# State-space heads: the parts of the third gate step all stand one pair of heads later

## The reference

```python
x = x + mamba2(gate0(x, f, f));  x = x + moe(gate1(x, f, f))
x = x + attention(gate2(x, f, f));  x = x + ffn(gate3(x, f, f))
```

```python
ek, ekv = exp(min(k, 30)), exp(min(k, 30)) * v
nf, df = scan forward of (ekv, ek) with a * decay + new      # along the 512 tokens
nb, db = the same scan backward
num = nf + nb - ekv + euk * v;  den = df + db - ek + euk     # euk = exp(min(u + k, 30))
out = sigmoid(r) * num / max(den, 1e-8) * (0.8 + 0.2 * tf)
```

```python
z, xBC, dt = split(u @ in_proj.T);  xBC = silu(conv4(xBC));  x, B, C = split(xBC)
L = tril(exp(cs_l - cs_s))            # per head, cs: running sum of dt * A in blocks
Y = (C B^T * L) (x dt) + C state * exp(cs) + x * D
y = Y * silu(z);  out = rmsnorm(y) * norm_w @ out_proj.T
```

## Time and profile before

| What | us |
|---|---|
| median of 3 runs | 2552.84 (2552.5 to 2559.88) |
| profiled execution, its own time | 2558.35 |
| its span in the trace | 2556.5 |
| DVE busy in the span | 1874.8 (73%) |
| PE busy in the span | 2282.6 (89%) |
| mean granted TensorE clock | 0.964 of full speed |

### The profile page before, as it was taken

One profiled execution on the slowest core, in us unless ns is written; L12 is line 12 of the kernel. 1 busy time (PEld: TensorE's weight loads), 2 busy tenths in 40 slices (PEclk: granted clock), 3 DMA queues, 4 the chain that ended last, 5 costly groups with the idle time before them and its releaser, 6 DMA issues.

```text
span 2556.5 us, 34018 instructions
## 1 busy us (share of the span) xinstructions
PE 2282.6 (89%) x10567; PEld 1688.2 (66%) x10568; DVE 1874.8 (73%) x2875; ACT 944.6 (37%) x1956; POOL 683.2 (27%) x545
## 2 busy tenths in 40 slices
PE   0789989989897899899878999999999988999998
PEld 0344444444455678778666888888888876788886
DVE  8989898889896765676545668768777785666665
ACT  3243342342432232342343444444434444322222
POOL 5434434343341443335331012122212210000000
PEclk9999999999998899999988999999999998999999
DMA  5000001010023432343241000010010101000001
GB/s 207 17 34 33 33 17 50 17 41 25 33 83 130 144 115 82 114 149 114 101 158 34 1 33 17 17 38 21 17 38 21 49 17 50 25 25 25 25 12 66
DMA packets 50502, 142.19 MB, mean 56 GB/s; under 512 B 4768, under 2 KB 4768, under 8 KB 46064
## 3 DMA queue, kind: packets, MB, share of 16 engines
q1 hardware_dynamic: 31872, 89.89, 10.0%
q10 hardware_dynamic: 12864, 32.81, 3.5%
q0 software_dynamic: 5680, 18.62, 2.4%
HBM read 106.95 MB, written 34.34 MB: 55 GB/s over the span
## 4 chain that ended last, share of the span: by engine, by line
PE 42%; issue 30%; POOL 10%; DVE 8%; POOLq 6%; ACT 3%; ACTq 0%; DMA 0%; DVEq 0%; another core or an unknown queue 0%
PE bank L341 9%; PE bank L343 9%; PE bank L342 9%; PE bank L2351 3%; PE bank L2352 3%; PE bank L2350 3%; PE bank L2304 3%; POOLq L494 2%; POOL g_v L495 2%; POOL g_v L502 2%; POOLq L520 1%; POOLq L517 1%; POOLq L506 1%; PE bank L2414 1%; POOL g_eu L501 1%
## 5 line engine op out<-in xcount | busy, mean ns | idle before, releaser
L2179 PE MATMUL bank<-um,w_in 128*128 128x512 f32 x576 | 263.5, 612 | 5.5 <-DVE lm L1515 5.3
L2179 PEld LDWEIGHTS bank<-um,w_in 128*128 128x128 f32 x576 | 110.0, 196 | 136.7 <-issue 128.5
L341 PE MATMUL bank<-u_hi,aw_hi 128*128 (+1 forms) x384 | 158.6, 413 | 12.9 <-DVE u_lo L1920 9.1
L1135 ACT ACTIVATE probs<-bank,nmx 128x128 f32<-128x128 f32 (+3 forms) x256 | 131.8, 528 | 91.6 <-DVE nmx L1943 91.6
L1142 ACT ACTIVATE pt_hi<-bank 128x512 fp32r<-128x512 f32 (+1 forms) x192 | 94.0, 526 | 165.0 <-PE bank L2304 163.8
L343 PE MATMUL bank<-u_hi,aw_lo 128*128 (+1 forms) x384 | 152.1, 396 | 0.0
L342 PE MATMUL bank<-u_lo,aw_hi 128*128 (+1 forms) x384 | 151.9, 396 | 0.0
L1958 DVE TENSOR_TENSOR pt_lo<-bank,pt_hi 128x512 fp32r<-128x512 f32 (+1 forms) x192 | 108.7, 593 | 42.5 <-ACT pt_hi L1142 41.1
L341 PE MATMUL bank<-u_hi,fw_hi 128*128 128x512 f32 x352 | 136.9, 389 | 0.0
L342 PE MATMUL bank<-u_lo,fw_hi 128*128 128x512 f32 x352 | 136.9, 389 | 0.0
L343 PE MATMUL bank<-u_hi,fw_lo 128*128 128x512 f32 x352 | 136.9, 389 | 0.0
(11 more groups left out here) (388 smaller groups left out, 6202.3 us busy)
## 6 DMA issues: line engine op xcount, KB each, us to landing
m_stage<-in_moe SPq DMA_DIRECT2D x21, 1024.0 KB, 5.3
y_slot<-m_o ACTq DMA_DIRECT2D x39, 256.0 KB, 2.7
g_v<-in_fT SPq DMA_DIRECT2D x18, 512.0 KB, 3.3
gates<-g_v SPq DMA_DIRECT2D x18, 512.0 KB, 2.8
f_stage<-in_ffn SPq DMA_DIRECT2D x11, 768.0 KB, 4.3
u_g<-gates SPq DMA_DIRECT2D x8, 1024.0 KB, 10.7
aw_in<-in_att SPq DMA_DIRECT2D x4, 1280.0 KB
w_in<-in_w_in ACTq DMA_DIRECT2D x1, 4640.0 KB, 16.8
```

Of the source, the lines that this page charges most:

```text
L341: nc.tensor.matmul(out, hi_w, hi_x, start=start, stop=False)
L1135: A(probs[:, h % 2, PR_AT[qb]:PR_AT[qb] + w], S_[bk][:, c0:c0 + w], ACT.Exp, bias=nmx[:, h % 2, qb:qb + 1], scale=SCALE, accum_out=rsum[:, ...
L2179: mm = M(dst[:], w_in[:, k, c0:c0 + P], um[:, k, :], start=(k == 0), stop=(k == KC - 1))
```

## The change

Each piece of the third gate step moves behind the output of the next pair of heads. The reciprocal, which stood behind pair 6, now stands behind pair 7, ahead of the two clamps of the fourth step, which stay where they were.

```diff
-                    if j == 0:
+                    if j == 1:
                         clamp(third, 0)
-                    elif j == 1:
+                    elif j == 2:
                         forward(third, 0)
                         clamp(third, 1)
-                    elif j == 2:
+                    elif j == 3:
                         backward(third, 0)
-                    elif j == 3:
+                    elif j == 4:
                         forward(third, 1)
-                    elif j == 4:
+                    elif j == 5:
                         backward(third, 1)
-                    elif j == 5:
+                    elif j == 6:
                         dens(third)
-                    elif j == 6:
+                    elif j == 7:
                         inverse(third)
-                    elif j == 7:
                         clamp(fourth, 0)
                         clamp(fourth, 1)
                 scans(fourth, 0)
```

## The result

The changed kernel takes **2590.62 us** (median of 4 runs, 2585.68 to 2593.72) against 2554.45 for the kernel before on the same chip (4 runs, 2552.5 to 2559.88): ratio 1.0137, 95% interval 1.0118 to 1.0156. Forecast were 2576.4 us and a range of 2567 to 2584. The direction was right, the size too small by more than the range allows.

The account below looks back on a forecast made before the run. DVE's own list was taken to bound each trip, PE's out_proj ending within 0.8 us of it; 5.9 us in each of four sequences, 23.6 us, on the 2552.84 us median gave 2576.4 us, range 2567 to 2584.

Parts of the forecast that it names:

- The chain in the loop: Each sequence's third to fourth gate step: the late reciprocal delays result, exponentials, products and scans, by 5.9 us a sequence.
- 4 x 5.9 = 23.6: Whole kernel: the 5.9 us delay counted in each of four sequences, 23.6 us added to the median.
- own range: Forecast case's range, 2571 to 2582 us, from the clamps' bounds and some 3 us of scatter; chance 0.74.
- the lower level does not fall on pair 2: Rival: PE finishes pair 2 at about 191.6, taking 1.6 us a sequence off: 17.2 us, 2570; chance 0.05.
- In the last sequence the same chain leads through the scans to the last additions to x, with which the mixture's routing begins: End of the last sequence: the delay there counts like the other three, 5.9 us.
- a wait of 3.4 us for DVE ahead of each *next trip: Trip's start: PE waits 3.4 us for DVE, so PE's own 1.7 us loss does not add.
- The rival on PE's clock: PE's clock falls in new gaps, slowing pair 7 by 1.5 us a sequence: 29.6 us, 2582; chance 0.07.
- The unknown at the clamps and POOL: Fourth step's clamp meeting POOL's first result: taken as zero more, bounds -0.3 and +0.7 us a sequence.
- The price of a meeting: POOL's result instruction meeting a DVE clamp: costs POOL 0.3 us or so, 1.61 us against 1.27.
- Faster, by the clamps: Rival at masked(2): tile 0's clamps gone, DVE gains 2.15 us a sequence plus a 0.53 us stall: -10.7 us, 2542; chance 0.05.

## Why the prediction was right in the loop and wrong in the sum

- *The chain in the loop* (DVE's stalls of 4.4, 2.2 and 1.8 us, the reciprocal 5.86 us late, 5.9 us a sequence): right. The stretch is 5.67 to 5.72 us longer in the first three and 6.03 in the fourth, 23.11 for 23.6. The reciprocal is 6.06 us late for 5.86, and the chain behind it, taken as unchanged at 9.31, is 0.41 us shorter. Moved alone, the reciprocal brings 4.12 of the 5.67; but the other pieces moved without it bring 3.95, so that it is not the reciprocal's place alone that counts.
- *"4 x 5.9 = 23.6"* as the loop's whole loss: 20.35 at the first token copy. The start came 1.13 us early, and PE's clock took 1.7 us off one of the trips. The own range had 3 us for such scatter, which is too little: the repetition of the changed kernel reached its first token copy 6.5 us earlier than the first profile (790.10 for 796.63), with three quick trips for one and two quick pairs 2 for none.
- *The rival "the lower level does not fall on pair 2"* had a chance of 0.05 for all four sequences, because two windows of one trace agreed. It is not an either-or: the changed kernel shows both, sequence by sequence.
- ***"In the last sequence the same chain leads through the scans to the last additions to x, with which the mixture's routing begins": this is the step that failed.*** It carried the delay into the routing as a shift and took the routing's own length for fixed. It grew from 31.8 to 45.7 us. The forecast had all that was needed: it found that out_proj moves by 1.7 us and DVE's list by 5.9, and put a wait of 3.4 us for DVE ahead of each *next trip*. The last sequence has no next trip; there the same wait stands ahead of the first token tile, and it measured 4.43 us. It was not priced, and with it went the 13.86 us: run with that gap bridged, the stretch took 31.9 us again.
- *The rival on PE's clock* named the mechanism but looked for it only in pair 7 and behind the trip's start, where PE's lead hides it (true: with that gap of 2.92 us, the stretch from the norm's reciprocal to the next output is 107.87 us for 107.82). Behind the last trip PE has no lead: its nine token tiles are on the chain that sets the end. With the 13.9 us that the trace measured, the sum would have been 2576.4 + 13.9 = 2590.3, for 2590.62. That it comes so close is luck in part: the loop's term was 3.2 us too high at the first token copy (20.35 for 23.6), and the kernel before ran 1.6 us above the 2552.84 from which the sum starts.
- *The unknown at the clamps and POOL*: taken as 0, and 0.08 us on L515 agrees. The price of a meeting was read from L516 at 221.09, beside which DVE also ran the last instruction of pair 7's output (L1619, 221.02 to 221.58), so the row doesn't single out the clamp. By the Trainium skill (SBUF — State Buffer, Who interferes with whom) whoever issues first blocks the other. The first clamp began 0.16 us ahead of L515 and took 0.39 us, so by that rule it would have held L515 for 0.23 us (an estimate); the row shows 0.08. The second clamp began behind L515 and took 1.49 us for 0.42 alone, ending 0.28 us behind L515's end: there the trace agrees, and DVE pays.
- *"Faster, by the clamps"*: the stall that ACT ends ahead of masked(2) was rightly held against it. Moving ACT's instruction and none of DVE's is what made a faster kernel, by 0.47%; the clamps of tile 0 stayed where they were in it. A kernel with both these clamps and ACT's exponentials moved, and the reciprocal in its place, was not run.

What stays open: why, after one and the same gap, the clock is high again in some executions and not in others. With a gap of 0.4 us all profiles were quick, with 4.4 us and no remedy all were slow, and between them (2.28 and 3.58) both happened; but the changed kernel with the exponentials later has the 4.43 us gap and four of its ten runs in the quick group. The traces show the order of events in each, not the chip's reason.

## What to carry to other kernels

Follow a delay past the loop's last trip: what waits there is another instruction, on another engine, and it may have no lead to hide the wait. Where fillers keep PE's clock up until a copy arrives, their number is right only for one clock and one arrival; a few us of idle time upstream can turn them from slow and long enough into fast and too short, so beside its own length, a new gap of PE is to be priced at the next run of matmuls on the path at half speed, as an end of the range. And a piece moved away from in front of a wait gains nothing if another engine ends that wait: look at that engine's instruction first.

## What the runs showed of the hardware

PE busy without a pause does not by itself get the full clock: at 30.00 of 30 us busy with 128-wide transposes, two fillers a tile and matmuls of 8 columns it stayed at 1.2 GHz, and the same work on other executions stayed at 2.4 GHz. In every profile these nine tiles kept the level with which they began. Behind a block of 12 or 16 fillers of 512 columns that began low it was high each time (5.28 and 5.33 us in the rows above). The Trainium skill (TensorE: Matmul & The Clock Gate, What's actually happening) has the array throttled by default and released by activity; by that rule the busy 30 us should have released it. They did not here, and the measurement decides.

A second place of this kind lies in the trip's middle, some 90 us behind the norm's reciprocal. The same four matmuls in two sequences of the changed kernel, from windows at a granted clock of 0.57 and 1.00, put 1.7 us between two trips (107.87 and 106.15 us from the norm's reciprocal to the next output of pair 0):

```profile
337.13 3.33 PE L2254 MATMUL bank<-state,b_tok 128*128 128x512 f32 x4
...
513.75 1.91 PE L2254 MATMUL bank<-state,b_tok 128*128 128x512 f32 x4
```

In the four profiles in which the loop up to the last sequence is that of the kernel before, all twelve trips took the longer time; in the other ten, 20 of 30 took the shorter. The twelve and the three of the kernel with the exponentials moved suggest that the kernel's own timing decides, not chance alone, but no run was made to show it.

The stretch from the maxima to the end, which no kernel here touches, took 1740 to 1749 us in the profiles. Differences under 5 us are therefore read better from the trace up to the maxima than from two times.
